# Fixed distances, period 15: re-timing the FFN jobs of a fused attention + FP4 FFN kernel

## What is computed

```python
x = inputs                                  # [4, 1024, 128] f32
xn = layernorm(x)
# attention: 16 heads of width 8, 1024 keys, linear position bias per head
scores = q @ k.T * scale + bias             # q, k, v = xn @ W + b
attn = softmax(scores)
a = (attn @ v) @ Wo + bo
# FFN, with every operand quantised in blocks of 16 to the FP4 grid
gate = fp4_linear(xn, w_gate)               # [., 352]
y = fp4_linear(xn, w_up)
f = fp4_linear(silu(gate) * y, w_down)      # back to [., 128]
out = x + a + f
```

## Time and profile before

| what | value |
|---|---|
| median of 3 runs | 842.89 us (842.72 to 843.2) |
| the profiled execution | 839.65 us, of which 837.8 us are its span |
| TensorE clock granted, mean over the span | 0.973 |
| TensorE busy (ends modelled) | 91% |
| VectorE busy | 83% |
| ScalarE busy | 78% |
| GpSimd busy | 50% |

### The profile page before, as it was taken

The page is one execution under the profiler, slowest core; times in us unless marked ns, Lnnn a source line. Parts: engine busy times, 40 slices in busy tenths (PEclk is TensorE's granted clock), DMA queues, the critical chain, the costliest instruction groups (busy, mean ns, idle before and its releaser), DMA issues.

```text
span 837.8 us, 13894 instructions
## 1 busy us (share of the span) xinstructions
PE 766.5 (91%) x4939; PEld 229.2 (27%) x4939; DVE 694.7 (83%) x794; ACT 650.3 (78%) x1340; POOL 415.4 (50%) x411
## 2 busy tenths in 40 slices
PE   3289999999999999899999999999999999999997
PEld 1012223222232333222232333222232323222223
DVE  7798888988988887888888887888988897989840
ACT  4206888877888888788878888888888888788886
POOL 7366263581729363771546462671716461362541
PEclk9657999999999999999999999999999999999999
DMA  5830002041102010050101002240101100000000
GB/s 150 243 59 2 2 2 78 2 117 36 39 2 52 2 51 28 18 149 2 40 2 39 3 1 90 89 77 2 39 2 27 27 14 2 2 2 2 2 2 26
DMA packets 32844, 31.85 MB, mean 38 GB/s; under 512 B 4360, under 2 KB 26568, under 8 KB 32776
## 3 DMA queue, kind: packets, MB, share of 16 engines
q1 hardware_dynamic: 32776, 30.96, 14.3%
HBM read 15.91 MB, written 15.04 MB: 37 GB/s over the span
## 4 chain that ended last, share of the span: by engine, by line
PE 70%; DVE 18%; ACT 7%; issue 3%; DMA 1%; SPq 1%; POOL 0%; ACTq 0%; POOLq 0%; DVEq 0%
PE low L1115 24%; PE mx L1085 22%; DVE neg_max L954 14%; PE low L1104 6%; ACT probs L748 4%; PE low L1153 3%; PE low L1132 3%; PE low L1138 2%; PE low L1071 2%; PE mx L1164 2%; ACT pv_s L845 2%; PE low L1145 1%; DVE am L925 1%; PE low L1179 1%; PE low L1067 1%
## 5 line engine op out<-in xcount | busy, mean ns | idle before, releaser
L954 DVE TENSOR_REDUCE neg_max<-mx 128x1 f32<-128x1024 f32 x512 | 613.9, 1220 | 94.0 <-PE mx L1085 85.6
L748 ACT ACTIVATE probs<-low 128x512 f32<-128x512 f32 x1007 | 550.6, 609 | 127.1 <-PE low L1104 121.3
L1085 PE MATMUL mx<-k_op,q_op 51*128 51x512 bf16 x1024 | 315.9, 393 | 40.8 <-DVE neg_max L954 20.9
L1104 PE MATMUL low<-q_op,k_op 53*128 53x512 bf16 x1007 | 325.4, 385 | 9.9 <-ACT probs L748 5.8
L1115 PE MATMUL low<-probs,v_op 128*32 128x512 f32 x2048 | 273.1, 605 | 1.9 <-ACT pv_s L845 1.1
L1085 PEld LDWEIGHTS mx<-k_op,q_op 51*128 51x128 bf16 x1024 | 61.6, 94 | 314.3 <-issue 176.5
L1104 PEld LDWEIGHTS low<-q_op,k_op 53*128 53x128 bf16 x1007 | 72.9, 93 | 81.4 <-ACT probs L748 71.6
L650 POOL CAST neg_parts<-neg_max 128x16 bf16<-128x16 f32 x31 | 6.8, 220 | 154.5 <-DVE neg_max L954 82.2
L557 POOL TENSOR_SCALAR mb<-mb 128x960 f32<-128x960 f32 (+2 forms) x17 | 58.7, 3456 | 26.9 <-DVE mb L945 25.6
L1115 PEld LDWEIGHTS low<-probs,v_op 128*32 128x32 f32 x2048 | 40.3, 108 | 68.4 <-issue 30.7
L638 POOL TENSOR_TENSOR x_s<-x_s,down_s 128x128 f32<-128x128 f32 x32 | 14.6, 456 | 74.4 <-ACT down_s L781 53.2
(11 more groups left out here) (138 smaller groups left out, 601.1 us busy)
## 6 DMA issues: line engine op xcount, KB each, us to landing
q_op<-q_rows SPq DMA_DIRECT2D x32, 192.0 KB, 3.9
k_op<-k_rows SPq DMA_DIRECT2D x32, 192.0 KB, 5.0
q_rows<-qp SPq DMA_DIRECT2D x8, 384.0 KB, 2.6
k_rows<-kp SPq DMA_DIRECT2D x8, 384.0 KB, 3.0
x_s<-in_L_attn_inputs_dram SPq DMA_DIRECT2D x8, 256.0 KB, 3.7
q_rows<-qp SPq DMA_DIRECT2D x8, 256.0 KB, 2.9
k_rows<-kp SPq DMA_DIRECT2D x8, 256.0 KB, 3.1
out_dram<-o_s SPq DMA_DIRECT2D x7, 256.0 KB, 2.4
```

The costliest lines, as they stand in the source:

```text
L748: nc.scalar.activation(probs[U % 3][:, 2 * g + x, :], bank("exp", U, j), ACT.Exp).then_inc(st_free, 1)
L954: nc.vector.tensor_reduce(to, slot("max", pos)[:], AX.X, ALU.max, negate=True).then_inc(mx_free, 1)
L1085: ins = nc.tensor.matmul(slot("max", pos)[:, 512 * kh:512 * kh + 512], q, k, start=True, stop=True)
L1104: nc.tensor.matmul(bank("exp", U, j), k_op[quad][r, g, kt * P:(kt + 1) * P], q_op[quad][r, g, half * HALF:(half + 1) * HALF], start=True, ...
```

## The change

The jobs of a pair now stand at fixed distances from its `xT` (the table `FROM_XT`), and a pair starts every 15 units instead of about every 15.5. Between the two `gate`, the two `up`, the two `hT` and the two `down` jobs there is now at least one unit. VectorE's and GpSimd's steps of the quantisation move with the `up` jobs and are one or two units later than they were behind them; VectorE's three maxima and `block_inverses` are now all behind a unit's second maximum. GpSimd runs `max_parts` one unit later in its program, at `turn_unit(m)`. `ctxT` and `wo` wait in the plan for the group's last `down`, and `wo` jobs have a unit between them. A semaphore of its own counts the last group's additions.

```diff
--- before.py
+++ after.py
@@ -72,7 +72,7 @@
 LEAD = 22
 CHUNKS = 2 * B * QUADS * UNITS
 HALVES = 2 * B * QUADS
-FFN_FIRST, FFN_LAST = 5, 237
+FFN_FIRST, FFN_STEP = 6, 15
 AT_END = ("turn", "pvT")
 IN_DVE_RING = ("pvT", "bvo")
 
@@ -108,7 +108,11 @@
 
 
 
-ROUNDED = 10
+
+
+FROM_XT = {("gate", 0): 2, ("gate", 1): 4, ("up", 0): 7, ("up", 1): 9, ("hT", 0): 23, ("hT", 1): 26,
+           ("down", 0): 28, ("down", 1): 31}
+ROUNDED = 13
 
 
 def norm_unit(b):
@@ -137,29 +141,26 @@
         if m >= LEAD // 16:
             put(turn_unit(m), "turn", m)
         put(KT * (m + 1) + (2 if m + 1 < HALVES else 1), "pvT", m)
-    x_at = put(FFN_FIRST, "xT", 0)
     for p in range(NP):
-        U = put(x_at + 1, "gate", p, 0)
-        U = put(U + 1, "gate", p, 1)
-        U = put(U + 2, "up", p, 0)
-        up = put(U + 1, "up", p, 1)
-        U = put(up + ROUNDED, "hT", p, 0)
-        U = put(U + 1, "hT", p, 1)
-        if p + 1 < NP:
-            x_at = put(FFN_FIRST + (FFN_LAST - FFN_FIRST) * (p + 1) // (NP - 1), "xT", p + 1)
-        U = put(U + 1, "down", p, 0)
-        put(U + 1, "down", p, 1)
+        start = FFN_FIRST + FFN_STEP * p
+        U = put(start, "xT", p)
+        for kind, t in FROM_XT:
+            U = U + (ROUNDED if (kind, t) == ("hT", 0) else 1)
+            if p + 1 < NP or kind in ("gate", "up"):
+                U = max(U, start + FROM_XT[kind, t])
+            U = put(U, kind, p, t)
     for b in range(1, B):
         for g in (2 * b, 2 * b + 1):
-            U = norm_unit(b) + 1 + 8 * (g % 2)
+            U = norm_unit(b) + 1 + 4 * (g % 2)
             for name in ("xnT", "q", "k"):
                 U = put(U + 1, name, g)
             assert U < parts_unit(g)
             put(max(U, QUADS * UNITS * (b - 1) + 2) + 1, "v", g)
+    U = 0
     for hb in range(2 * B):
-        U = put(at["pvT", hb // 2 * 8 + 6 + hb % 2] + 1, "ctxT", hb)
+        U = put(max(U, at["pvT", hb // 2 * 8 + 6 + hb % 2], at["down", 2 * hb + 1, 1] - 1) + 1, "ctxT", hb)
         for i in range(2):
-            U = put(max(U, at["down", 2 * hb + 1, 1]) + 1, "wo", hb, i)
+            U = put(max(U, at["down", 2 * hb + 1, 1]) + 1 + i, "wo", hb, i)
     return at
 
 
@@ -329,6 +330,7 @@
         hid_ok = sem("hid_ok")
         down_ok = sem("down_ok")
         out_ok = sem("out_ok")
+        last_out_ok = sem("last_out_ok")
         z_ok = sem("z_ok")
         pow_ok = sem("pow_ok")
         quant_ok = sem("quant_ok")
@@ -456,7 +458,10 @@
 
             def store(g, t0, t1):
                 i = g % 2
-                sp.wait_ge(out_ok, 2 * g + t1 * 2 // GT)
+                if g + 1 < NG:
+                    sp.wait_ge(out_ok, 2 * g + t1 * 2 // GT)
+                else:
+                    sp.wait_ge(last_out_ok, t1 * 2 // GT)
                 sp.dma_start(out_tok[g * GT + t0:g * GT + t1].rearrange("t p e -> p t e"),
                              o_s[i][:, t0 * P:t1 * P].rearrange("p (t e) -> p t e", e=E)).then_inc(stored[i], 16)
 
@@ -661,7 +666,7 @@
             for U in range(NU + 2 * KT):
                 b, u = divmod(U, QUADS * UNITS)
                 for m in range(1, HALVES):
-                    if U == turn_unit(m) - 1:
+                    if U == turn_unit(m):
                         max_parts(m)
                 if u == 2 and b < B:
                     add_bias(b)
@@ -676,13 +681,13 @@
                         add_wo(job[1], job[2])
                 for p in range(NP):
                     up = AT["up", p, 1]
-                    if U == up + 3:
+                    if U == up + 5:
                         scale_to_grid(p + 1)
-                    if U == up + 5:
+                    if U == up + 7:
                         add_power(p + 1)
-                    if U == up + 7:
+                    if U == up + 9:
                         take_power(p + 1)
-                    if U == up + 8:
+                    if U == up + 10:
                         scale_back(p + 1)
                 for g in range(2, NG):
                     if U == norm_unit(g // 2):
@@ -1005,7 +1010,7 @@
                 dve.wait_ge(down_ok, 2 * NP)
                 dve.wait_ge(stored[hb % 2], (hb // 2 + 1) * 16)
                 nc.vector.tensor_tensor(to, bank("wo", hb, i)[:, 0:PW], x_s[:, hb * GW + i * PW:hb * GW + (i + 1) * PW],
-                                        ALU.add).then_inc(out_ok, 1)
+                                        ALU.add).then_inc(last_out_ok, 1)
 
             for U in range(NU + 2 * KT):
                 for i in range(2):
@@ -1021,15 +1026,15 @@
                         up0, up1 = AT["up", p, 0], AT["up", p, 1]
                         if (U, i) == (up0 + 1, 1):
                             x_maxima(p + 1)
-                        if (U, i) == (up0 + 2, 0):
+                        if (U, i) == (up0 + 2, 1):
                             hidden_maxima(p + 1, 0)
-                        if (U, i) == (up1 + 2, 0):
+                        if (U, i) == (up1 + 2, 1):
                             hidden_maxima(p + 1, 1)
-                        if (U, i) == (up1 + 2, 1):
+                        if (U, i) == (up1 + 3, 1):
                             block_scales(p + 1)
-                        if (U, i) == (up1 + 3, 0):
+                        if (U, i) == (up1 + 4, 1):
                             block_inverses(p + 1)
-                        if (U, i) == (up1 + 4, 1):
+                        if (U, i) == (up1 + 6, 1):
                             powers(p + 1)
                 for job in end(U):
                     job_on_vector(job)
```

## The result

The changed kernel takes **836.73 us** (median of six executions, 832.99 to 838.19) against 842.94 us (842.31 to 843.5) for the kernel before, a ratio of 0.9922 with a 95% interval of 0.9902 to 0.9942. The forecast was 836.6. First the page: busy times by engine, then the chain that ended last by engine (before: the earlier trace rows).

The account below looks back on a forecast made before the run. TensorE, busy 91% of the span, was taken to set the pace, with 9.8 us lost waiting for VectorE. Terms: -0.7 - 9.8 + 1.3 + 3.0 + 0.4 - 0.5 = -6.3, from 842.9 to 836.6 us; range 832.3 to 842.1.

Parts of the forecast that it names:

- the largest term: VectorE's extra steps move behind jobs, so its lag in jobless stretches no longer holds up TensorE: -9.8 us.
- Counts of jobs, and unit 245's: Two fewer jobs meet the `pv_s` copy, -0.7 us; unit 245's job is gone, so the last `turn` comes earlier, -0.5.
- The debt before: In the kernel before, VectorE falls behind in jobless stretches and TensorE waits: 9.8 us, 0.65 for each of 15 pairs.
- Debt gone, +1.3 back: VectorE's 9.8 us of lag goes; +1.3 returns from `powers`, the scales and pair 0's steps in jobless units 17 to 19.
- From `turn` to the scores that need it 4.3 us go by ... there are at least 5.4: Every `turn` but the last leaves at least 5.4 us before its scores, which need 4.3.
- Two late turns: At turns 7 and 22 GpSimd's split stands behind `add_power`, so TensorE waits 1.5 us each: +3.0.
- The turns with 0.5 to spare: Turns 9 and 24, with `add_power` and an `add_down` ahead of the split, pass: 7.7 us against some 8.3.
- The split one unit later costs and gains nothing else: GpSimd's split of the maxima no longer delays a due `hid` step, but room existed in both kernels: counted as nothing.
- `powers` at 0.65, scales slowed in one pair: VectorE's `powers` no longer takes 1.39 beside GpSimd's `three_parts`; `block_scales` may lose up to 0.7 once or twice: +0.2.
- The end: Five jobs instead of four between unit 248 and 255, where ScalarE is the pace: +0.4 us for one `hT` copy.
- the room isn't usable: Rival, chance 0.15: steps behind job units push the next jobless unit, 7.5 of the 9.8 us come back: 842.8 us.
- slower: late turns: Rival, chance 0.10: GpSimd's split is late at more turns, 1.5 us each; nine late turns give 847 us.

Follow-up runs that it names:

- experiment 2: Changed kernel with GpSimd's split of the row maxima one unit earlier for turns 7 and 22 alone: 833.14 us, ratio 0.9865 to the kernel before.
- experiment 3: Kernel before with only GpSimd's split of the row maxima one unit later, for all turns: 848.62 us, ratio 1.0057.
- experiment 1: Changed kernel with GpSimd's split of the row maxima back one unit earlier for all 31 turns: 834.7 us, ratio 0.9884 to the kernel before.
- experiment 4: Changed kernel with VectorE's two hidden_maxima, block_scales and block_inverses back at their old distances from the up jobs: 837.47 us, ratio 0.993 to the kernel before.
- experiment 6: Changed kernel plus seven unused 0.51 us VectorE reductions, each in a unit with a job: 836.08 us, ratio 0.9929 to the kernel before.
- experiment 7: Changed kernel plus seven unused 0.51 us VectorE reductions, each in a jobless unit: 835.17 us, ratio 0.991 to the kernel before.
- experiment 8: Changed kernel with early splits for turns 7 and 22, plus three 0.51 us VectorE reductions at once in seven jobless units: 839.89 us.
- experiment 9: Changed kernel with early splits for turns 7 and 22, plus 21 VectorE reductions of 0.51 us, one per unit: 834.44 us.
- experiment 10: Changed kernel's plan of jobs alone, with VectorE's and GpSimd's steps and the split at their old distances: 838.42 us, ratio 0.9922 to the kernel before.
- experiment 5: Kernel before with its old planner, but the steps at the new distances for all pairs except the last: 837.74 us, ratio 0.9938.

## Why the prediction was right, point by point

The total was right, and so was each term's sign. The reason I gave for the largest term was only partly so, and that 836.6 came within 0.2 of 836.73 is luck: errors of 0.5 us and more cancelled, as the points show, and the executions of the changed kernel alone differ by 5 us.

- *Counts of jobs, and unit 245's* (-0.7 and -0.5): -1.15 smooth and +0.05 in units 246 to 248, so -1.10 for -1.2. The new job of unit 247 is hidden in the wait for the last turn's DMAs, as said.
- *The debt before* (9.8): 9.77 by the table, but my way to it had two errors that cancelled. The group at 813.77 is unit 249's, and that of 248 is at 810.74, so I had 3.0 too much time; and the last three units, which have none of the `mx` half products left, take 5.7 in all, where I had the smooth 7.4 and 1.4 more, 3.1 too much again. One made the debt larger, the other smaller.
- *Debt gone, +1.3 back* (-8.5): -8.70 measured. Jobless units are at 2.46 to 2.50 and the steps stand one to a unit, but not each with a pause behind it. The +1.3 was placed wrongly: unit 19 has 0.08, where I had 0.3. What came back is 0.27 to 0.31 in units 44, 56 and 204, and 0.48 in unit 216, which I hadn't foreseen (next point).
- *"From `turn` to the scores that need it 4.3 us go by ... there are at least 5.4"*: this step failed, at the price of 0.48 in the changed kernel's profile. The chain of the changed kernel behind `turn` 27:

```profile
709.92 0.08 PE low L1098
...
710.28 0.02 issue
710.30 3.20 DMA m_rows<-max_t
...
714.03 1.70 DMA q_op<-m_rows
715.73 0.05 issue
715.78 0.39 PE low L1109
```

  The first transfer took 3.20, where the last turn's takes 1.35, so the scores that were due 5.6 behind the `turn` of 709.73 came 6.05 behind it, and unit 216 was held up. Before, the same transfer took 2.77, and the scores were due only 6.0 behind their turn (712.23 to 718.28), with nothing longer. The same step fails at turn 23: its transfer took 2.70 here and cost nothing, but 2.8 to 3.3 in the experiments with this plan, and there unit 184 was held up by 0.1 to 0.6. In experiment 2:

  ```profile
  617.35 0.09 PEld L1109 LDWEIGHTS low<-q_op,k_op 53*128 53x128 bf16 x1 [0.34 <-DMA q_op<-m_rows]
  ```
- *Two late turns* (+3.0, 1.5 each): 2.86, 1.43 each, at turns 7 and 22 and nowhere else. `add_power` lasts from 222.39 to 228.14 and the split to 228.70, the 5.7 and 0.5 of the sum. The turns with 0.5 to spare passed.
- *The split one unit later costs and gains nothing else*: right on the gain. That a late turn can also drop the clock (experiment 3) was not in the sum.
- *`powers` at 0.65, scales slowed in one pair*: `powers` is 0.65 for all 14 tiles of 128x960, and no 1.39 is left. One `sc`, at 351.91, took 0.39 instead of 0.18; before, two did (0.36 and 0.41), so this isn't a new cost.
- *The end* (+0.4): +0.96 in this execution; in experiments 1, 2, 4 and 6 to 10, which have the same plan at the end, it is +0.3 to +0.8 (27.37 to 27.85).
- *The rival "the room isn't usable"*, 842.8: wrong, and in the opposite direction. **A jobless unit has more room than I gave it.** VectorE waits 0.4 for TensorE ahead of its first maximum after a unit with a job, and it may start the next one later than that without anyone waiting. In experiment 7 the maximum behind the extra step begins 0.88 into unit 102 instead of 0.67, the interval takes 2.49, and VectorE is back on time in the next. In experiment 5 TensorE's second pair of `mx` products, which follows VectorE's maxima, begins 0.60, 0.60 and 0.97 into units 46 to 48 instead of 0.45, and these take 2.49, 2.46 and 2.50 (only `powers` falls there); before, with four of the steps there, it begins at 1.26, 1.16 and 1.32, and they take 2.79, 2.69 and 2.84. So about one step of 0.5 can be behind at no cost. What lies beyond is paid at least in part: three steps of together 1.36 cost 0.4 to 0.9. Before, the six steps had eight maxima between the first and the last and, where the stretch was jobless, no unit in which to make up. The new plan gives the time back between them, and is enough for most of it (experiment 10). The new distances put more maxima between them, and do the same in the two pairs of experiment 5 where nothing else changed.
- *The rival "slower: late turns"*: not with this plan, but it is what the same edit does to the old one (experiment 3).

The median of the prediction came from adding 3.2 to the profiled time. I had no reason for it. The profiled execution of before is one that reached unit 1 early (70.80), and a start one level later (last section) would be about the 3.2; the other executions have no trace, so this isn't shown.

What stays open: the 0.27 in units 44 and 204, whose jobs are an `hT` and a `ctxT`, and the 0.31 in unit 56, which is gone when the two splits are early, were not tried.

## What to carry to other kernels

Where one engine has both a steady duty and occasional extra steps, don't count room unit by unit: take how far behind it may fall before another engine waits, and ask that each step is made up before the next. A wait that a planner's table moves is found by listing, for each hand-over, what its engine has ahead of it in the unit before; a step of 0.4 us behind one of 5.7 is late even when the engine is busy only half of the time. When a change has several parts, try each alone: here one part cost 2.8 of the 9 us that the others brought, and the version without it takes 833.14 instead of 836.73.

## What the runs showed of the hardware

**The clock after a pause.** Windows in experiment 6 around `turn` 22, where TensorE stood idle for 1.24 us:

```profile
594.00:596.00 2.00, 1.15 (x8) 0.43 (x8) 0.36 (x1) 0.76 (x3) 1.43 (x5) 1.00 0.00 0
596.00:598.00 2.00, 1.89 (x10) 0.25 (x11) 1.99 (x2) 1.56 (x4) 1.92 (x2) 0.71 0.02 4
598.00:600.00 2.00, 2.00 (x10) 0.63 (x6) 0.93 (x1) 1.08 (x2) 1.81 (x2) 0.50 0.06 12
600.00:605.00 5.00, 4.88 (x35) 0.92 (x34) 4.21 (x5) 4.00 (x9) 3.53 (x2) 0.97 0.33 74
```

The granted clock went from 1.00 to 0.50, that is from 2.4 to 1.2 GHz, and the interval of unit 175 took 1.51 more, on top of the 1.42 of the wait. Experiment 4 has the same at the same place. The profiled execution of the changed kernel has a pause of 1.25 at turn 7 with the clock at 1.00 behind it. So such a pause sometimes costs double. Whether this is why the changed kernel's executions spread over 5 us (832.99 to 838.19) is open: those of experiment 2, without the pauses, spread over 0.8, but those of experiment 1, also without them, over 4.5. The start levels below move an execution by as much.

**GpSimd and VectorE at the start.** Unit 1's group starts at one of three levels, 70.4 to 70.9, 73.4 to 74.6 or 76.8 to 77.2, and the same code is found at different ones. VectorE's timeline of the changed kernel at the first place:

```profile
13.24 3.73 DVE L905 CAST probs<-probs 16x1024 bf16<-16x1024 f32 x1
```

and GpSimd's beside it:

```profile
12.81 0.94 POOL L528 MEMSET k_op<- 128x1024 f32 x1
13.70 0.94 POOL L529 MEMSET q_op<- 128x1024 f32 x1
```

In the kernel before the same CAST took 1.05, and GpSimd's MEMSET took 1.49:

```profile
13.23 1.05 DVE L900 CAST probs<-probs 16x1024 bf16<-16x1024 f32 x1
```

```profile
13.68 1.49 POOL L524 MEMSET q_op<- 128x1024 f32 x1
```

That is 2.7 us. The second place is VectorE's own split for `turn` 0: `neg_parts` took 3.64 in experiment 1, starting at 61.61 together with a `take_power` of GpSimd that took 3.62, and 0.17 in experiment 7:

```profile
61.61 3.64 DVE L963 TENSOR_TENSOR neg_parts<-neg_max,neg_parts 128x16 bf16<-128x16 f32 x1
```

```profile
58.40 0.17 DVE L968 TENSOR_TENSOR neg_parts<-neg_max,neg_parts 128x16 bf16<-128x16 f32 x1
```

Of the twelve kernels profiled, the long CAST is in seven and the long `neg_parts` in five, with both plans among either, so neither belongs to the change. The Trainium skill (SBUF, State Buffer, section "Who interferes with whom") says that the engine that issues first holds the shared port pair for its whole instruction and the other blocks fully, and that a `tensor_tensor` with both inputs in SBUF contends with GpSimd's reads: the 3.64 beside the 3.62 agrees. The same section of the Trainium skill says that a reduction never contends on this chip. The maxima kept their mean of 1.22 before and after, which agrees, but they read the `mx` slots and not SBUF, so it is a weak test.

**A small transfer with two durations.** `m_rows<-max_t`, 8 KB, takes some 1.35 at most turns and 2.7 to 3.3 at some (turns 7, 15, 23 and 27 in the changed kernel, 7, 10, 15, 18 and 27 in the one before), with one in between in each (turn 26 and turn 8). I didn't find out why. With 3.2 for it the scores come 6.05 behind the turn, and a plan that leaves less pays the difference.
